# Self-attention of a decoder layer: the outputs' trailing bits move from POOL to VectorE, behind a round's maxima

## What is computed

```python
def _L0_attn_ref(x, wq, wk, wv, wo):        # N_HEADS = 16, HEAD_DIM = 64
    xq = jnp.einsum('bsh,oh->bso', x, wq)
    xk = jnp.einsum('bsh,oh->bso', x, wk)
    xv = jnp.einsum('bsh,oh->bso', x, wv)
    xq = xq.reshape(bsz, N_HEADS, seqlen, HEAD_DIM)
    xk = xk.reshape(bsz, N_HEADS, seqlen, HEAD_DIM)
    xv = xv.reshape(bsz, N_HEADS, seqlen, HEAD_DIM)
    scores = jnp.einsum('bhid,bhjd->bhij', xq, xk) * SCALE
    scores = jax.nn.softmax(scores, axis=-1)
    out = jnp.einsum('bhij,bhjd->bhid', scores, xv)
    out = out.reshape(bsz, seqlen, N_HEADS * HEAD_DIM)
    return jnp.einsum('bso,ho->bsh', out, wo)
...
x = x + _L0_attn_ref(_layernorm(x, axis=-1), wq, wk, wv, wo)
```

## Time and profile before

| | |
|---|---|
| median of 3 runs (lowest to highest) | 1658.84 us (1657.04 to 1662.4) |
| profiled execution, its own time | 1658.88 us |
| its span, first to last instruction | 1657.1 us |
| mean granted TensorE clock | 0.941 |
| busy: TensorE / VectorE / ScalarE / POOL | 87% / 58% / 46% / 34% of the span |
| self-attention | about the first 673 us |

### The profile page before, as it was taken

One profiled execution on the slowest core, in us unless ns is written; L12 is line 12 of the kernel. 1 busy time (PEld: TensorE's weight loads), 2 busy tenths in 40 slices (PEclk: granted clock), 3 DMA queues, 4 the chain that ended last, 5 costly groups with the idle time before them and its releaser, 6 DMA issues. The chain is left out here.

```text
span 1657.1 us, 39281 instructions
## 1 busy us (share of the span) xinstructions
PE 1446.5 (87%) x12244; PEld 1250.0 (75%) x12244; DVE 962.8 (58%) x2371; ACT 760.2 (46%) x1830; POOL 563.7 (34%) x692
## 2 busy tenths in 40 slices
PE   4789899999999998479999999999986119999997
PEld 3688878888887877368888888888866118888886
DVE  5547475656566665157777777767653215555553
ACT  4547464655555565035655555555651002222221
POOL 5244353525252617512222222222202443333332
PEclk9899999999999999679999999999995559999999
DMA  5703030303021221387676666767621413555551
GB/s 180 208 2 81 1 79 2 77 13 66 17 62 34 45 44 37 78 216 193 179 198 180 189 186 184 199 176 200 172 73 53 143 57 126 188 184 189 180 182 51
DMA packets 159950, 195.71 MB, mean 118 GB/s; under 512 B 83724, under 2 KB 128307, under 8 KB 159636
## 3 DMA queue, kind: packets, MB, share of 16 engines
q1 hardware_dynamic: 154356, 186.09, 40.6%
q0 software_dynamic: 3968, 6.59, 1.2%
q10 hardware_dynamic: 1568, 2.30, 0.5%
HBM read 138.63 MB, written 58.05 MB: 119 GB/s over the span
## 5 line engine op out<-in xcount | busy, mean ns | idle before, releaser
L1209 DVE TENSOR_REDUCE row_max<-psb_s 100x1 f32<-100x361 f32 x512 | 263.4, 531 | 140.1 <-PE psb_s L1352 134.2
L1101 ACT ACTIVATE probs<-psb_t 121x400 f32<-121x400 f32 (+1 forms) x384 | 190.5, 508 | 115.2 <-PE psb_t L1362 112.5
L1352 PE MATMUL psb_s<-k,q 97*100 97x362 f32 x512 | 185.3, 364 | 15.2 <-DVE row_max L1209 9.4
L437 POOL TENSOR_TENSOR diag<-neg_ident,row_max 100x400 fp32r<-100x400 f32 x128 | 112.2, 898 | 183.0 <-DVE row_max L529 158.2
L1362 PE MATMUL psb_t<-q,k 98*121 98x200 f32 (+1 forms) x768 | 147.5, 274 | 1.9 <-ACT probs L1101 1.7
L2032 PE MATMUL psd_h<-h_in,w_sb 128*128 128x256 f32 x640 | 144.2, 384 | 1.4 <-ACT h_in L1898 1.4
L2040 PE MATMUL psd_y<-w_sb,hid 128*128 128x256 f32 x640 | 144.5, 379 | 0.0
L2032 PEld LDWEIGHTS psd_h<-h_in,w_sb 128*128 128x128 f32 x640 | 123.5, 193 | 19.0 <-issue 1.8
L2040 PEld LDWEIGHTS psd_y<-w_sb,hid 128*128 128x128 f32 x640 | 120.1, 190 | 15.5
L1362 PEld LDWEIGHTS psb_t<-q,k 98*121 98x121 f32 (+1 forms) x768 | 125.4, 184 | 6.1 <-ACT probs L1101 2.7
L1352 PEld LDWEIGHTS psb_s<-k,q 97*100 97x100 f32 x512 | 85.7, 168 | 41.5 <-DVE row_max L1209 27.2
(11 more groups left out here) (226 smaller groups left out, 3604.6 us busy)
## 6 DMA issues: line engine op xcount, KB each, us to landing
w_sb<-in_w SPq DMA_DIRECT2D x40, 1024.0 KB, 7.6
packed_keys<-k_st SPq DMA_DIRECT2D x32, 724.0 KB, 3.5
k<-packed_keys SPq DMA_DIRECT2D x64, 362.0 KB
v_rows<-v_tok SPq DMA_DIRECT2D x32, 400.0 KB
v_ext<-v_rows SPq DMA_DIRECT2D x32, 400.0 KB
q<-packed_queries SPq DMA_DIRECT2D x64, 200.0 KB
k<-packed_keys SPq DMA_DIRECT2D x64, 181.0 KB
c_t<-in_contextT SPq DMA_DIRECT2D x32, 361.0 KB, 4.6
```

The source lines that it names most:

```text
L437: pool.tensor_tensor(diag[:, g % 2], c.neg_ident[0:S, 0:S].unsqueeze(1).to_broadcast([S, GH, S]), row_max[:, g // 2 % 2, g % 2].unsqueeze( ...
L1101: act.activation(probs[0:KT[kt], u % 2, kt], ps_t[i % 2][0:KT[kt], 0:4 * S], ACT.Exp, scale=HD2 ** -0.5).then_inc(probs_ready, 1)
L1209: dve.reduce_max(row_max[:, p, h:h + 1], ps_s[h % 2][0:S, 0:S2], AX_X).then_inc(max_ready, 1)
L1352: pe.matmul(ps_s[h % 2][0:S, 0:S2E], q2[0:97, p, u, g, S * a:S * (a + 1)], k2[0:97, p, u, g], start=True, stop=True).then_inc(scores_ready, 1)
```

## The change

POOL makes o_hi only. VectorE makes o_lo, in passes 3 to 10, right behind its maxima (in passes 8 to 10, where there are none, first of all), and ahead of the reciprocals and o_norms of the pass. It waits for o_hi of the same round.

```diff
+        def ordered(r):
+            s0 = SQ * (r % GB)
+            return (o_part[:, r % 2].rearrange("p g (s t) -> p g t s", t=NT), o_hi[:, :, :, s0:s0 + SQ],
+                    o_lo[:, :, :, s0:s0 + SQ])
...
             def split_outputs(q, r):
-                s0 = SQ * (r % GB)
-                hi, lo = (t[:, :, :, s0:s0 + SQ] for t in (o_hi, o_lo))
-                src = o_part[:, r % 2].rearrange("p g (s t) -> p g t s", t=NT)
+                src, hi, _ = ordered(r)
                 pool.wait_ge(ot_copied_act, q * 2 * GQ + 4 * (r + 1))
                 if r % GB == 0:
                     reach(pool, y_ready, q * QUAD + 2 * (r // GB))
                 pool.sem_inc(pool_passed, 1)
                 pool.tensor_copy(hi, src).then_inc(o_hi_ready, 1)
-                pool.wait_ge(o_hi_ready, q * ROUNDS + (r + 1))
-                pool.tensor_tensor(lo, src, hi.bitcast(F32), ALU.subtract).then_inc(o_lo_ready, 1)
...
                                            "p h (g j) -> p h g j", g=2), AX_X).then_inc(max_ready, 1)
+                    if r >= 3:
+                        src, hi, lo = ordered(r - 3)
+                        dve.wait_ge(o_hi_ready, q * ROUNDS + (r - 2))
+                        dve.tensor_tensor(lo, src, hi.bitcast(F32), ALU.subtract).then_inc(o_lo_ready, 1)
                     for f in values_in(r):
                         values_out(q, f)
                     for g in in_round(r - 2):
```

## The result

| | before | changed |
|---|---|---|
| median, us | 1657.94 (4 runs, 1653.13 to 1662.4) | 1736.42 (4 runs, 1730.65 to 1745.94) |
| ratio, 95% interval | | 1.0476 (1.0424 to 1.0528) |
| profiled execution: time, span | 1658.88, 1657.1 | 1730.65, 1728.9 |
| mean granted clock | 0.941 | 0.912 |

The change makes the kernel 78 us slower. The profile after comes from the fastest of its four runs, 72 us over the profiled execution before.

The account below looks back on a forecast made before the run. TensorE was taken to bound self-attention. Longer turn-to-turn waits, less gains at the projections, gave 7 x 6.5 + 9.4 = 55 us on 1658.9, so 1714 us, range 1694 to 1744.

Parts of the forecast that it names:

- The ring: Self-attention passes: turns, ScalarE's copies, POOL's o_hi, VectorE's o_lo, o_norms, next turns; plus 1.63 us a pass.
- case A: Self-attention: the new turn-to-turn wait sets the pace, 1714 us, 1695 to 1742 by the bounds; chance 0.76.
- Its length: From the second group's turns to the next pass's: 5.25 us against 3.62 a pass; 3.87 to o_lo's end.
- The sum of the ring: Over eight quads of self-attention: 6.5 us for each of seven, 9.4 for the last, 55 us in all.
- The gains at the projections: Passes 6 and 10: shorter waits for o_lo; pass 6 gives back 1.33 us, leaving about 0.4 of wait.
- The clock: TensorE in self-attention: falls to 1.2 GHz cost little, inside time it waits anyway; nothing put in the sum.
- Case C: Self-attention: TensorE's clock falls far more often, two unhidden falls more a quad, 24 us, 1738 us; chance 0.08.
- The signs: In the profile: some 50 turn waits of 1.3 to 1.8 us, o_lo idle 1.3 before; clock under 0.95 throughout means clock rival.
- The port: Memory port shared by VectorE and POOL: whichever comes first keeps the other out; diagonals expected to wait, with slack.
- case B: Passes 3 to 7: POOL's diagonals get in first, each o_lo waits 0.83 us, 33 us more, 1747; chance 0.10.
- The price of the step: VectorE's o_lo, reading with a step of eight words: 0.86 us from L264's copies, bounds 0.57 and 1.29.

Follow-up runs that it names:

- experiment 1: Changed kernel with VectorE's o_lo moved behind the o_norms of the pass: 1654.33 us, ratio 0.9975 to the kernel before.
- experiment 5: Changed kernel with five unused TensorE products ahead of the turns in passes 3, 4, 5 and 7: 1700.23 us, ratio 1.0250 to the kernel before.
- experiment 4: Changed kernel with o_lo made twice in a row on VectorE, a semaphore between the two: 1797.96 us.

## Why the prediction was right, and where it was off

The direction and the main cause were right. The time was inside the range by luck: two errors of opposite sign made it so.

- **The ring** (case A) is shown. Its place: experiment 1 moves one instruction behind four others and 82 us are gone. Its arithmetic: turns 4.13 us apart without o_lo, 5.0 to 5.1 with it, and 0.96 us for each o_lo more.
- **Its length** was put at 5.25 us and is 5.0 to 5.1. The part up to the end of o_lo was right, 3.8 to 3.9 us against 3.87, with errors that cancel: o_lo was priced at 0.86 and took 0.90 on average, the first copy started up to 0.50 us behind the second pair of turns and not 0.43, the step from ScalarE to POOL was 0.17 and not 0.24 (525.57 to 525.74), that from POOL to VectorE 0.03 and not 0.08. The error lies behind o_lo. The two reciprocals and o_norms took 1.19 us (527.53 to 528.72), not 1.28, and the first of them starts 0.08 us before the end of o_lo in the profile (527.53 against 527.61), where I had it 0.04 behind. In the kernel before, the second reciprocal came late for a reason of its own (it started at 484.60, right behind the end of TensorE's products at 484.56), and I took that gap for part of the work.
- **The sum of the ring** was therefore too high: 55 us forecast, 42 us measured with the clock held up. A middle quad took 83.8 us in experiment 5 (the additions to x behind pass 10 at 373.88 and 457.64) against 78.4 before, 5.4 us and not 6.5; the last took 7.6 us more and not 9.4. Seven of the one and one of the other are 45 us, and about 4 go off for the three falls that only the kernel before has.
- **The gains at the projections** are there, in pass 6 more than forecast. I had said about 0.4 us of wait left for each (my own sum leaves 0.30); at full clock it is 0.14 to 0.20, and none in the quads that come there at 1.2 GHz. o_lo ends as long behind the turns as I had it. It is TensorE that arrives later: its second pair of turns waits for the second o_norm, and the next scores start 0.29 us behind that pair (533.83 to 534.12) and not 0.12 (482.36 to 482.48).
- **The clock** is the step that failed: "I put nothing for it in the sum", because a fall would only run into time that TensorE waits anyway. It cost 36 us. One short fall does cost little, but at 1.2 GHz a pass takes 6.64 us where the ring takes 5.0 to 5.1, so TensorE has more to do than the wait can hide, and the low clock lasts: of the changed kernel's low stretches five held for 14 to 20 us. Case C had 1738 us for the time, close to the 1736.42 measured, but as 24 us on top of 55; it was 36 on top of 42. The forecast of 1714 is 22 us low. With the ring as long as I had it, the clock's 36 us would have made some 1750, outside the range.
- **The signs** that I had named mix A and C. The turns wait for VectorE's o_norm 43 times, but for 29.1 us in all, 0.7 each and 1.4 at most, not 1.3 to 1.8: a part of the wait is inside the four turns, and at 1.2 GHz there is none. o_lo has 1.6 us of idle time before it on average, in the pass shown 1.04. The clock was under 0.95 in six of the nine stretches, not throughout.
- **The port** (case B) did not cost what it could have. o_lo was never held back in the changed kernel (0.87 to 0.95 us each). It held back POOL: the diagonals of pass 3 took 2.05 us in place of 1.66. That is the exclusion of the earlier trace rows, with o_lo first, as forecast. By the Trainium skill (SBUF — State Buffer, Who interferes with whom) it is whoever comes first, and the trace agrees in both directions: with a second o_lo in experiment 4, which starts when the diagonals already run, it is VectorE's that takes 1.28 in place of 0.88 us.
- **The price of the step** by row L264 (0.86 us) was nearer to the 0.90 measured than either price of the Trainium skill (Vector Engine (DVE) Microarchitecture Reference, 5.2 Measured stream behaviour on trn2), 0.77 and 1.08 as an estimate. The two bracket it. The higher one rests on 2.50 ns a column, which that page gives for a step of 24 words on both sources or on the destination, not on one source as here. The step of eight words costs 0.82 ns more an element, (0.904 - 0.576) / 400.

## What to carry to other kernels

When work moves to an engine that has time to spare, look first at what is queued behind it there and at what it waits for: if the queued work feeds the chain that the wait comes from, the two close into a ring, and its length is the new pace, whatever the busy shares say. Put such an instruction behind everything that the bounding engine waits for; here that turned 1736 us into 1650. And count the second price of a new wait on TensorE, its clock: here waits of about 1 us in every pass took the granted clock down for 14 to 20 us at a time, and where that happens, products that nobody needs can be faster than waiting.

## What was not expected of the hardware

- TensorE's clock fell although TensorE never waited longer than 1.4 us for an o_norm, once every 5 us. Of its ten low stretches between 100 and 660 us nine began at most 2.4 us behind the start of turns that had waited 0.7 to 1.2 us for an o_norm, and one behind the wait of 1.92 us for o_lo. In other quads of the same execution the same passes stayed at full clock (the stretch from 480 to 540 us above, 0.98). What decides between the two was not settled.
- Products without a use made the kernel faster twice, by 36 us in the ring and by 9.4 us in one wait of 2 us a quad.
